# Another order of the attention slot's parts on three engines, and a rearranged prologue

## The chip, the cores and the metric

The kernel runs on one core of a Trainium2 chip. The time is the device time in microseconds of one execution. Five engines run from queues of their own and wait for each other on semaphores: TensorE (PE) does the matmuls into PSUM, VectorE (DVE), ScalarE (ACT) and GpSimd (POOL) work element by element, and SyncE (SP) issues DMAs.

## The reference

It is one transformer-like block on x of shape (2, 1024, 128): attention with 16 heads of 64, a feed-forward layer, a second attention with one head and a distance bias, and the feed-forward layer again. Each has a layer norm ahead and is added to x.

```python
q = einsum('bse,hed->bhsd', x, Wq) + bq      # k, v alike
scores = einsum('bhsd,bhtd->bhst', q, k) / sqrt(64)
scores = where(causal, scores, -inf)
out = einsum('bhst,bhtd->bhsd', softmax(scores), v)
return out.transpose(0, 2, 1, 3).reshape(B, S, H * 64) @ Wo + bo

x = x + attn_a(layernorm(x))
x = x + ffn(layernorm(x))     # relu(x @ w1 + b1) @ w2 + b2
x = x + attn_b(layernorm(x))
x = x + ffn(layernorm(x))
```

## The kernel before

Each engine has its queue written out by hand, and semaphores that only count up tie them together. The order in which the code of an engine stands is the order in which it runs; nothing is reordered.

The change touches the prologue and the first attention. This attention has 32 heads (2 batches x 16), and the kernel goes through one of them in each slot: `pe_slot(u)`, `act_slot(u)` and `dve_slot(u)` say what PE, ACT and DVE do in slot u, for u from 0 to 31; POOL runs `low(u, r)` nine times a slot, and SP moves the pieces. A slot mixes work on several heads:

- scores of head u, `scores(u, r)`: the causal part of the 1024x1024 scores comes in nine units of 512 columns, r = 0 to 8, each in one PSUM bank out of a ring of three. Numbers are split in a high and a low part, so a unit takes two matmuls for each of its parts, and a small one more with the mask where a part lies on the diagonal.
- exponentials of head u, `exponentials(u, r)` on ACT: each unit is read twice, into `p32` in f32 (a ring of four) and into the high part of `p_hl` in f16. POOL subtracts them for the low part (`low`, L1534). `scores` waits for the exponentials three units earlier.
- outputs of head u-1, `products(step)` on PE: nine steps of 12 matmuls, into two groups of four query tiles each; `outputs(0)` and `outputs(1)` on DVE divide the groups by their sums (`outputs_out`). The first group is full after step 2, the second after step 8.
- maxima of head u+1, `maximum(n)`: eight query tiles, the longest (1024 keys) first. PE fills PSUM (`max_tile`, L523) and DVE takes the row maxima (`take_max`, L1126). The five tiles of 512 keys and more come one by one through the same banks, so PE can fill the next only when DVE is done with the one before; the last three alternate between two banks. When all are done, PE turns the maxima (`turn_maxima`, L538) and DVE spreads them into rows of `q_hm` (`max_rows`, L1133), for which the next slot's scores wait.
- a projection for a later pair of heads, `project(half)`: a piece of K or Q, three f32 matmuls of 512 columns into the bank `MISC`; ACT makes the high part (`piece_high`, L911), DVE the low one (`piece_low`, L1109), and SP moves both to their places. Slots 0 to 28 have two pieces each. In slots 1 to 28 a unit of V follows (`value_unit`, `value_high`, `value_low`) in the same bank, behind both pieces.

Of the input's four chunks, two are normalised and turned in the prologue. Chunks 2 and 3, which only heads of the second batch need, are late: `LATE_CHUNKS = (2, 3)`, and `late_chunk(u, step)` gives the chunk whose turn it is in slot u. Their statistics, normalisation (`chunk_norm`, L1094, on DVE), turn on PE (`turn_chunk`, L490) and the split into `xT_hi` (ACT) and `xT_lo` (DVE) stand in the slots. `turn_maxima` also waits for the split of a late chunk, since both use bank 7.

The prologue loads the weights, scales and splits their first quarter, makes pieces 0 to 3 and four units of V, then pieces 4 and 5 (K of the second pair of heads), the maxima of head 0, and, in the middle of them, eight products of a column of bias with Wo (L685). ACT casts and POOL subtracts the other three quarters of the weights; PE waits for that (`rest_lo`) before slot 0. After slot 31 come the output projection, the feed-forward layer, the second attention and the last layer.

## Time and profile before

| | |
|---|---|
| median of 3 runs | 646.46 us |
| lowest, highest | 642.22, 647.32 us |
| the profiled execution | 647.31 us |
| its span in the profile | 645.0 us |
| mean granted clock of PE | 0.957 |
| PE, DVE, ACT, POOL busy | 88%, 75%, 71%, 62% |

The span runs from the first to the last instruction; the execution's own time holds 2.3 us more around it. All rows below are of this one execution, and their times count from the span's start. The busy shares are means over stages of different kinds: prologue to 47.66, slots to about 470, the rest to the end.

### The profile page before, as it was taken

To read this page: it belongs to the slowest core of one execution; us is meant where nothing else is said; L and a number is where in the kernel's file an instruction comes from. 1 tells how busy PE (TensorE), PEld (TensorE's weight loads), DVE (VectorE), ACT (ScalarE), POOL (GpSimd) and SP (SyncE) were. 2 spreads that over 40 slices of the span, in tenths; PEclk is the share of its full clock that TensorE was granted. 3 is DMA by queue.
4 is the path that set the end of the run, shared out by engine and by line. 5 is a ranking of instruction groups with operands and counts; after the bars stand their busy time and mean duration, and the time that the engine had idled before them with its cause. 6 is when DMAs were issued, how large, how long until landed. Compare 5 with 4: busy or idle time off the path is not lost.

```text
span 645.0 us, 16576 instructions
## 1 busy us (share of the span) xinstructions
PE 565.8 (88%) x6230; PEld 414.0 (64%) x6230; DVE 481.3 (75%) x1450; ACT 457.8 (71%) x869; POOL 397.0 (62%) x376
## 2 busy tenths in 40 slices
PE   1668998978999999999999999999799998799697
PEld 1534766645666666766666676666588776577575
DVE  6446878877887787878778887887248799678774
ACT  3447887757878887888888888888745685156375
POOL 3275787856777887788778878888920142045410
PEclk9868999979999999999999999999999999689799
DMA  9422243222322323234233333340754000000001
GB/s 229 98 49 51 51 107 75 66 64 62 96 63 83 91 76 100 58 100 108 51 98 77 90 86 74 85 107 3 246 183 169 0 2 1 0 1 3 1 16 51
DMA packets 35327, 47.88 MB, mean 74 GB/s; under 512 B 10776, under 2 KB 16688, under 8 KB 35248
## 3 DMA queue, kind: packets, MB, share of 16 engines
q1 hardware_dynamic: 33136, 46.29, 26.3%
q8 instruction: 50, 0.82, 0.6%
q10 hardware_dynamic: 2112, 0.54, 0.4%
q14 instruction: 29, 0.24, 0.1%
HBM read 12.21 MB, written 9.44 MB: 34 GB/s over the span
## 4 chain that ended last, share of the span: by engine, by line
PE 35%; ACT 22%; issue 16%; DVE 14%; POOL 10%; DMA 2%; SPq 0%; POOLq 0%; ACTq 0%; DVEq 0%
POOL p_hl L1534 9%; ACT p L975 8%; ACT p_hl L976 7%; PE psum L479 5%; PE psum L481 5%; PE psum L480 4%; PE psum L523 3%; ACT v_all L921 3%; DVE v_all L1116 3%; DVE xn L1094 2%; PE psum L578 2%; PE psum L579 2%; PE psum L558 2%; PE psum L560 2%; PE psum L559 2%
## 5 line engine op out<-in xcount | busy, mean ns | idle before, releaser
L1534 POOL TENSOR_TENSOR p_hl<-p,p_hl 128x512 f16<-128x512 f32 x288 | 326.0, 1161 | 90.5 <-ACT p_hl L976 87.3
L1126 DVE CUSTOM_DVE_ANT_0 max_junk<-psum,mask_s 128x1024 bf16<-128x1024 f32 (+7 forms) x256 | 190.0, 753 | 62.1 <-issue 57.6
L975 ACT ACTIVATE p<-psum 128x512 f32<-128x512 f32 x288 | 179.4, 623 | 16.7 <-PE psum L581 13.4
L976 ACT ACTIVATE p_hl<-psum 128x512 f16<-128x512 f32 x288 | 181.2, 629 | 0.0
L523 PE MATMUL psum<-k_hh,q_hl 128*128 128x512 f16 (+3 forms) x384 | 108.2, 338 | 31.0 <-DVE maxima L1126 30.7
L558 PE MATMUL psum<-v_all,p_hl 128*128 128x65 f16 x1152 | 125.5, 193 | 3.6 <-POOL p_hl L1534 3.6
L559 PE MATMUL psum<-v_all,p_hl 128*128 128x64 f16 x1152 | 125.6, 193 | 0.0
L578 PE MATMUL psum<-q_hl,k_hh 128*128 128x512 f16 (+3 forms) x384 | 125.1, 330 | 0.3 <-DVE q_hm L1133 0.2
L560 PE MATMUL psum<-v_all,p_hl 128*128 128x65 f16 x1152 | 125.1, 195 | 0.0
L579 PE MATMUL psum<-q_hm,k_l 128*128 128x512 f16 (+3 forms) x384 | 123.0, 329 | 0.0
L558 PEld LDWEIGHTS psum<-v_all,p_hl 128*128 128x128 f16 x1152 | 107.9, 99 | 11.9 <-POOL p_hl L1534 4.0
L559 PEld LDWEIGHTS psum<-v_all,p_hl 128*128 128x128 f16 x1152 | 107.1, 98 | 8.0
L560 PEld LDWEIGHTS psum<-v_all,p_hl 128*128 128x128 f16 x1152 | 107.2, 97 | 0.0
L911 ACT ACTIVATE st_hi<-psum,b_kq 128x512 f16<-128x512 f32 x64 | 44.1, 689 | 73.3 <-PE psum L481 63.4
L523 PEld LDWEIGHTS psum<-k_hh,q_hl 128*128 128x128 f16 x384 | 29.1, 98 | 64.5 <-DVE maxima L1126 57.7
L1109 DVE SCALAR_TENSOR_TENSOR st_lo<-psum,b_kq,st_hi 128x512 f16<-128x512 f32 x64 | 47.9, 748 | 26.6 <-ACT st_hi L911 26.6
L578 PEld LDWEIGHTS psum<-q_hl,k_hh 128*128 128x128 f16 x384 | 37.7, 98 | 34.3 <-ACT p_hl L976 15.6
L581 PE MATMUL psum<-mask_t,ident_b 128*128 128x128 bf16 x256 | 53.5, 221 | 0.0
L479 PE MATMUL psum<-xT_hi,w_hi 128*128 128x512 f32 x96 | 46.4, 483 | 5.7 <-DVE w_lo L1247 3.5
L1489 POOL TENSOR_SCALAR var_eps<-mean_var 128x4 f32<-128x4 f32 x16 | 5.4, 340 | 73.3 <-DVE mean_var L1083 73.3
L579 PEld LDWEIGHTS psum<-q_hm,k_l 128*128 128x128 f16 x384 | 37.9, 99 | 8.8 <-issue 0.3
L1575 POOL TENSOR_TENSOR p_hlb<-p32b,p_hlb 128x512 f16<-128x512 f32 x18 | 21.0, 1173 | 35.4 <-ACT p_hlb L1068 35.4
(184 smaller groups left out, 1131.8 us busy)
## 6 DMA issues: line engine op xcount, KB each, us to landing
k_hh<-st_hi SPq DMA_DIRECT2D x64, 128.0 KB, 2.4
o_scratch<-o_sb SPq DMA_DIRECT2D x16, 512.0 KB, 3.1
o_in<-o_scratch SPq DMA_DIRECT2D x4, 2048.0 KB, 7.9
k_l<-st_lo SPq DMA_DIRECT2D x32, 128.0 KB, 2.4
q_hl<-st_hi SPq DMA_DIRECT2D x32, 128.0 KB, 2.3
q_hl<-st_lo SPq DMA_DIRECT2D x32, 128.0 KB, 2.3
q_hm<-st_hi SPq DMA_DIRECT2D x32, 128.0 KB, 2.3
x_sb<-in_L_attn_a_x SPq DMA_DIRECT2D x4, 256.0 KB, 4.1
```

Source lines behind the costliest of these rows:

```text
L479: nc.tensor.matmul(dst, hi, m_hi, start=start, stop=False)
L523: last = nc.tensor.matmul(max_banks(j, c0, c1), q_hl[:, s, P * j:P * (j + 1)], k_hh[:, s, c0:c1], start=True, stop=True)
L558: nc.tensor.matmul(dst, p_hl[:, par, 0, cols], v_hi_one, start=(kt == 0), stop=False)
L559: nc.tensor.matmul(dst[:, 0:DH], p_hl[:, par, 0, cols], v_lo, start=False, stop=False)
L560: last = nc.tensor.matmul(dst, p_hl[:, par, 1, cols], v_hi_one, start=False, stop=(kt == j))
L578: nc.tensor.matmul(dst, k_hh[:, s, keys], q_hl[:, s, q0:q0 + n], start=True, stop=False)
L579: last = nc.tensor.matmul(dst, k_l1[:, s, keys], q_hm[:, s, q0:q0 + n], start=False, stop=not diagonal)
L581: last = nc.tensor.matmul(dst[:, 0:P], ident_b[:, :], mask_t[:, :], start=False, stop=True)
L975: nc.scalar.activation(p32[:, ring_at(u, r), :], src, ACT.Exp, scale=SCALE_A).then_inc(exp_done, 1)
L976: nc.scalar.activation(p_hl[:, u % 2, 0, BANK * r:BANK * (r + 1)], src, ACT.Exp, scale=SCALE_A).then_inc(phi_done, 1)
L1126: nc.vector.tensor_tensor_reduce(out=max_junk[:, n % 2, 0:cols], in0=max_banks(j, 0, cols), in1=mask_s[:, S - cols:S], scale=1.0, scalar=- ...
L1534: nc.gpsimd.tensor_tensor(p_hl[:, u % 2, 1, cols], p32[:, ring_at(u, r), :], p_hl[:, u % 2, 0, cols], ALU.subtract)\
```

## The change

- The order of the parts within `pe_slot`, `act_slot` and `dve_slot` is another. On DVE `max_rows` now stands ahead of `outputs(1)`, and `outputs(0)` ahead of maximum 2.
- The late chunks are normalised on ACT: x times rstd plus a shift of -mean times rstd, which POOL makes (`chunk_shift`). Statistics come in slots 1 and 2, POOL's part in 2 and 3, `late_norm` in 4 and 5, turn and split in 5 and 6 (before: statistics at the starts of slots 4 and 5, normalisation at those of 6 and 7, turn and split in 6 and 7).
- In the prologue, the bias products stand behind the units of V and go to bank 6; pieces 4 and 5 stand between maxima 1, 2 and 3 of head 0; on ACT their high parts come behind the four units of V. SP loads the late chunks of x ahead of the feed-forward weights.

```diff
@@ -356,7 +358,7 @@
 
             return min(u + FIRST_UNITS, VUNITS)
 
-        def late_chunk(u, step=4):
+        def late_chunk(u, step=3):
 
             return u - step if u - step in LATE_CHUNKS else None
 
@@ -400,12 +402,12 @@
             sp.dma_start(w_raw[:, 2, :].rearrange("p (h d) -> p h d", h=H), Wv.rearrange("h e d -> e h d")).then_inc(wv_in, 16)
             sp.dma_start(wo_raw[:, :, :], Wo.rearrange("(k p) e -> p k e", p=P)).then_inc(wo_in, 16)
             sp.dma_start(bo_sb[:, :], bo.unsqueeze(1)).then_inc(bo_in, 16)
+            load_x(2)
+            load_x(3)
             sp.dma_start(w1_raw[:, :], w1).then_inc(ffn_in, 16)
             sp.dma_start(w2_raw[:, :, :], w2.rearrange("(m p) e -> p m e", p=P)).then_inc(ffn_in, 16)
             sp.dma_start(b1_sb[:, :], b1.rearrange("(m p) -> p m", p=P), allow_slow_non_contiguous=True).then_inc(ffn_in, 16)
             sp.dma_start(b2_sb[:, :], b2.unsqueeze(1)).then_inc(ffn_in, 16)
-            load_x(2)
-            load_x(3)
 
             sp.wait_ge(piece_lo, 2)
             move_k(0)
@@ -546,6 +548,7 @@
                         if j == 0:
                             pe.wait_ge(v_lo_done, units_for(w))
                             pe.wait_ge(v_one, 1)
+                            pe.wait_ge(bo_done, 1)
                         if j == 0 or need_units[j] > need_units[j - 1]:
 
                             pe.wait_ge(plo_done, NU * w + need_units[j])
@@ -614,36 +617,36 @@
                         turn_maxima(u + 1)
 
                 products(0)
+                products(1)
                 maximum(0)
-                products(1)
                 project(0)
                 scores(u, 0)
+                scores(u, 1)
                 maximum(1)
-                scores(u, 1)
+                products(2)
                 scores(u, 2)
                 project(1)
                 maximum(2)
-                products(2)
                 products(3)
-                products(4)
-                products(5)
-                maximum(3)
                 scores(u, 3)
                 scores(u, 4)
+                maximum(3)
                 scores(u, 5)
                 value_unit()
                 maximum(4)
-                products(6)
                 maximum(5)
+                products(4)
+                products(5)
                 scores(u, 6)
                 maximum(6)
+                products(6)
                 if late_chunk(u) is not None:
                     pe.wait_ge(v_lo_done, units_after(u))
                     turn_chunk(late_chunk(u))
+                scores(u, 7)
+                maximum(7)
                 products(7)
-                maximum(7)
                 products(8)
-                scores(u, 7)
                 rows()
                 scores(u, 8)
 
@@ -669,22 +672,18 @@
                 if m < 3:
                     pe.wait_ge(piece_lo, m + 2)
                 values(m, V_BANKS[m])
-
-            for n in range(4, 6):
-                pe.wait_ge(piece_lo, n)
-                piece(n, MISC)
+            pe.wait_ge(wo_in, 16)
+            for k in range(OB):
+                last = nc.tensor.matmul(bank(6)[:, 0:1], wo_raw[:, k, :], b_cols[:, 2, k:k + 1], start=(k == 0), stop=(k == OB - 1))
+            last.then_inc(bo_full, 1)
+
             pe.wait_ge(k_moved[0], 48)
             pe.wait_ge(q_moved[0], 48)
             for n in range(QT):
                 max_tile(0, n)
-                if n == 3:
-
-                    pe.wait_ge(wo_in, 16)
-                    pe.wait_ge(piece_lo, 6)
-                    for k in range(OB):
-                        last = nc.tensor.matmul(bank(MISC)[:, 0:1], wo_raw[:, k, :], b_cols[:, 2, k:k + 1], start=(k == 0), stop=(k == OB - 1))
-                    last.then_inc(bo_full, 1)
-            pe.wait_ge(bo_done, 1)
+                if n in (1, 2):
+                    pe.wait_ge(piece_lo, n + 3)
+                    piece(n + 3, MISC)
             turn_maxima(0)
             pe.wait_ge(rows_ready, 1)
             pe.wait_ge(tri_ready, 2)
@@ -899,6 +898,16 @@
                 c = n % CHUNKS
                 nc.scalar.copy(xT_hi[:, BANK * c:BANK * (c + 1)], xt_bank(n)).then_inc(xt_hi_done, 1)
 
+            def late_norm(n):
+
+                act.wait_ge(shift_done, n - LATE_CHUNKS[0] + 1)
+                act.wait_ge(xt_full, n - 1)
+                for j in range(CT):
+                    tile = CT * n + j
+                    last = nc.scalar.activation(xn[:, n % 2, j, :], x_sb[:, tile, :], ACT.Identity, bias=shift[:, tile:tile + 1],
+                                                scale=rstd[:, tile:tile + 1])
+                last.then_inc(xn_ready, 1)
+
             def piece_high(n, src=MISC):
 
                 pair, which, half = n // 4, n % 4 // 2, n % 2
@@ -950,9 +959,8 @@
                 act.wait_ge(v_full, m + 1)
                 nc.scalar.copy(p32[:, m, :], bank(V_BANKS[m])).then_inc(v32_done, 1)
                 value_high(m, V_BANKS[m])
-                if m == 1:
-                    for n in range(4, 6):
-                        piece_high(n)
+            for n in range(4, 6):
+                piece_high(n)
             for which, dst in enumerate((w_hi[:, 0, :], w_hi[:, 1, :], wv_hi[:, :])):
                 act.wait_ge(rest_scaled, which + 1)
                 nc.scalar.copy(dst[:, FIRST:], w_raw[:, which, FIRST:]).then_inc(rest_hi, 1)
@@ -983,9 +991,11 @@
 
                 project(0)
                 exponentials(u, 0)
-                project(1)
                 exponentials(u, 1)
                 exponentials(u, 2)
+                project(1)
+                if late_chunk(u, 2) is not None:
+                    late_norm(late_chunk(u, 2))
                 exponentials(u, 3)
                 exponentials(u, 4)
                 if unit_in(u) is not None:
@@ -1168,27 +1178,25 @@
                         outputs_out(u - 1, g)
 
                 maximum(0)
+                if late_chunk(u, -1) is not None:
+                    first_stats(late_chunk(u, -1))
                 project(0)
                 maximum(1)
+                outputs(0)
                 maximum(2)
                 project(1)
                 maximum(3)
-                outputs(0)
                 maximum(4)
+                maximum(5)
                 if unit_in(u) is not None:
                     value_low(unit_in(u))
-                maximum(5)
+                if late_chunk(u) is not None:
+                    chunk_low(late_chunk(u))
                 maximum(6)
                 maximum(7)
-                if late_chunk(u) is not None:
-                    chunk_low(late_chunk(u))
-                outputs(1)
                 if u + 1 < HEADS:
                     max_rows(u + 1)
-                if late_chunk(u, 1) is not None:
-                    first_stats(late_chunk(u, 1))
-                if late_chunk(u, 3) is not None:
-                    chunk_norm(late_chunk(u, 3))
+                outputs(1)
 
             nc.vector.memset(minus_half[:, :], -0.5).then_inc(half_ready, 1)
             nc.vector.memset(ones[:, :], 1.0).then_inc(ones_ready, 1)
@@ -1265,23 +1273,23 @@
             for n in range(2):
                 piece_low(n, FIRST_BANKS[n])
             norm_v()
-            for n in range(2, 4):
-                piece_low(n, FIRST_BANKS[n])
+            piece_low(2, FIRST_BANKS[2])
             gain_v()
+            piece_low(3, FIRST_BANKS[3])
             dve.wait_ge(inv_done, 2)
             first_low(2)
             for which in range(3):
                 rest_scale(which)
-            for n in range(4, 6):
-                piece_low(n)
             dve.wait_ge(tri_ready, 2)
             for n in range(QT):
                 take_max(0, n)
+                if n in (1, 2):
+                    piece_low(n + 3)
                 if n == 5:
 
                     dve.wait_ge(bo_in, 16)
                     dve.wait_ge(bo_full, 1)
-                    nc.vector.tensor_tensor(bo_all[:, :], bank(MISC)[:, 0:1], bo_sb[:, :], ALU.add).then_inc(bo_done, 1)
+                    nc.vector.tensor_tensor(bo_all[:, :], bank(6)[:, 0:1], bo_sb[:, :], ALU.add).then_inc(bo_done, 1)
             dve.wait_ge(diag_ready, 1)
             dve.wait_ge(qm_zeroed, 1)
             max_rows(0)
@@ -1490,6 +1498,14 @@
                 pool.wait_ge(eps_done, n + 1)
                 nc.gpsimd.tensor_tensor(rstd[:, cols], var_eps[:, cols], minus_half[:, :], ALU.pow).then_inc(rstd_done, 1)
 
+            def chunk_shift(n):
+
+                cols = slice(CT * n, CT * (n + 1))
+                nc.gpsimd.tensor_scalar(shift[:, cols], mean_var[:, cols, 0], -1.0, None, ALU.mult).then_inc(mean_turned, 1)
+                pool.wait_ge(mean_turned, n - LATE_CHUNKS[0] + 1)
+                pool.wait_ge(rstd_done, n + 1)
+                nc.gpsimd.tensor_tensor(shift[:, cols], shift[:, cols], rstd[:, cols], ALU.mult).then_inc(shift_done, 1)
+
             pool.wait_ge(half_ready, 1)
             chunk_rstd(0)
             chunk_rstd(1)
@@ -1537,8 +1553,9 @@
             for u in range(HEADS):
                 for r in range(NU):
                     low(u, r)
-                    if r == 4 and late_chunk(u, 2) is not None:
-                        chunk_rstd(late_chunk(u, 2))
+                    if r == 4 and late_chunk(u, 0) is not None:
+                        chunk_rstd(late_chunk(u, 0))
+                        chunk_shift(late_chunk(u, 0))
 
 
             pool.wait_ge(o_ready, NG * HEADS)
```

Where the order moves is shown at three places of steady slots. The same statements stand 2 to 10 lines further down in the changed kernel. On PE, the rows from the first projection of slot 8 on: `w_hi` and `w_lo` are in the projection, L523 (now L525) is a maximum fill, L578, L579 and L581 (now L581, L582 and L584) are the two matmuls and the mask of scores. Before:

```order
L479 MATMUL psum<-xT_hi,w_hi 128x512
L480 MATMUL psum<-xT_hi,w_lo 128x512
L481 MATMUL psum<-xT_lo,w_hi 128x512
L578 MATMUL psum<-q_hl,k_hh 128x512
L579 MATMUL psum<-q_hm,k_l_81 128x512
L581 MATMUL psum<-mask_t,ident_b 128x128
L523 MATMUL psum<-k_hh,q_hl 128x512
L523 MATMUL psum<-k_hh,q_hl 128x384
L578 MATMUL psum<-q_hl,k_hh 128x384
L579 MATMUL psum<-q_hm,k_l_81 128x384
L581 MATMUL psum<-mask_t,ident_b 128x128
```

And now, from the end of the same projection on:

```order
L483 MATMUL psum<-xT_lo,w_hi 128x512
L581 MATMUL psum<-q_hl,k_hh 128x512
L582 MATMUL psum<-q_hm,k_l_82 128x512
L584 MATMUL psum<-mask_t,ident_b 128x128
L581 MATMUL psum<-q_hl,k_hh 128x384
L582 MATMUL psum<-q_hm,k_l_82 128x384
L584 MATMUL psum<-mask_t,ident_b 128x128
L581 MATMUL psum<-q_hl,k_hh 128x128
L582 MATMUL psum<-q_hm,k_l_82 128x128
L584 MATMUL psum<-mask_t,ident_b 128x128
L525 MATMUL psum<-k_hh,q_hl 128x512
L525 MATMUL psum<-k_hh,q_hl 128x384
```

The fill of maximum 1 (512 and 384 columns) stood behind score unit 0, and now stands behind unit 1.

On PE again, the end of the slot, around the last maximum fill (128 columns) and score unit 7 (512 columns and the mask). Before, from the last output matmul of the slot to the turn of the maxima (L538):

```order
L560 MATMUL psum<-v_all,p_hl 128x65
L578 MATMUL psum<-q_hl,k_hh 128x512
L579 MATMUL psum<-q_hm,k_l_81 128x512
L581 MATMUL psum<-mask_t,ident_b 128x128
L538 MATMUL psum<-ident,maxima 8x128
```

And now, from the same unit of scores to the first of the 24 output matmuls that follow:

```order
L581 MATMUL psum<-q_hl,k_hh 128x512
L582 MATMUL psum<-q_hm,k_l_82 128x512
L584 MATMUL psum<-mask_t,ident_b 128x128
L525 MATMUL psum<-k_hh,q_hl 128x128
L561 MATMUL psum<-v_all,p_hl 128x65
```

Score unit 7 stood between the last output group and the turn of the maxima; now it stands ahead of the last fill, and two groups of 12 output matmuls stand between that fill and the turn.

On DVE, the boundary of two slots, from the last maximum to the first of the next head. Before:

```order
L1126 ISA max_junk,maxima<-psum,mask_s 128x128
L1126 ISA maxima 128x1
L1144 RECIPROCAL o_den<-psum 128x4
L1153 TENSOR_TENSOR o_sb<-psum,o_den 128x4x64
L1133 TENSOR_TENSOR q_hm<-psum,neg_diag 8x1024
L1125 MEMSET gate 128x1
L1126 ISA max_junk,maxima<-psum,mask_s 128x1024
L1126 ISA maxima 128x1
L1109 SCALAR_TENSOR_TENSOR st_lo<-psum,b_kq,st_hi 128x512
```

And now:

```order
L1136 ISA max_junk,maxima<-psum,mask_s 128x128
L1136 ISA maxima 128x1
L1143 TENSOR_TENSOR q_hm<-psum,neg_diag 8x1024
L1154 RECIPROCAL o_den<-psum 128x4
L1163 TENSOR_TENSOR o_sb<-psum,o_den 128x4x64
L1135 MEMSET gate 128x1
L1136 ISA max_junk,maxima<-psum,mask_s 128x1024
L1136 ISA maxima 128x1
L1119 SCALAR_TENSOR_TENSOR st_lo<-psum,b_kq,st_hi 128x512
```

The rows `q_hm` of the next head stood behind the second output group (`o_den`, `o_sb`), and now stand ahead of it.

## Rows read from the trace of the kernel before

**Rows 1.** The page, busy us (share of the span) and instructions of an engine.

```profile
PE 565.8 (88%) x6230; PEld 414.0 (64%) x6230; DVE 481.3 (75%) x1450; ACT 457.8 (71%) x869; POOL 397.0 (62%) x376
```

**Rows 2.** Timeline of DVE, runs of `max_rows`: start, duration, engine, line, output, inputs.

```profile
47.66 1.22 DVE L1133 TENSOR_TENSOR q_hm<-psum,neg_diag 8x1024 f16<-8x1024 f32 x1 [0.61 <-PE psum L538]
60.55 1.22 DVE L1133 TENSOR_TENSOR q_hm<-psum,neg_diag 8x1024 f16<-8x1024 f32 x1 [0.37 <-PE psum L538]
...
126.79 1.22 DVE L1133 TENSOR_TENSOR q_hm<-psum,neg_diag 8x1024 f16<-8x1024 f32 x1
147.32 1.22 DVE L1133 TENSOR_TENSOR q_hm<-psum,neg_diag 8x1024 f16<-8x1024 f32 x1
163.01 1.22 DVE L1133 TENSOR_TENSOR q_hm<-psum,neg_diag 8x1024 f16<-8x1024 f32 x1
175.74 1.22 DVE L1133 TENSOR_TENSOR q_hm<-psum,neg_diag 8x1024 f16<-8x1024 f32 x1
...
431.45 1.22 DVE L1133 TENSOR_TENSOR q_hm<-psum,neg_diag 8x1024 f16<-8x1024 f32 x1
442.08 1.22 DVE L1133 TENSOR_TENSOR q_hm<-psum,neg_diag 8x1024 f16<-8x1024 f32 x1
```

**Rows 3.** Timeline of PE in a steady slot; in brackets idle time and releaser.

```profile
202.74 0.48 PE L479 MATMUL psum<-xT_hi,w_hi 128*128 128x512 f32 x1
...
203.53 0.39 PE L578 MATMUL psum<-q_hl,k_hh 128*128 128x512 f16 x1
...
204.02 0.54 PE L523 MATMUL psum<-k_hh,q_hl 128*128 128x512 f16 x2
...
210.55 0.19 PE L558 MATMUL psum<-v_all,p_hl 128*128 128x65 f16 x1
...
210.92 0.32 PE L523 MATMUL psum<-k_hh,q_hl 128*128 128x384 f16 x1
...
211.63 0.19 PE L558 MATMUL psum<-v_all,p_hl 128*128 128x65 f16 x1
...
212.79 0.23 PE L523 MATMUL psum<-k_hh,q_hl 128*128 128x128 f16 x1 [0.63 <-DVE maxima L1126]
```

**Rows 4.** Timeline of DVE: statistics; fifth maximum of a steady slot.

```profile
100.38 0.87 DVE L1079 BATCH_NORM_STATS2 stats<-x_sb 128x6 f32<-128x128 f32 x4
...
210.76 0.69 DVE L1126 CUSTOM_DVE_ANT_0 max_junk<-psum,mask_s 128x512 bf16<-128x512 f32 x1 [0.77 <-issue]
```

**Rows 5.** Timeline of POOL in the steady slot.

```profile
208.25 1.16 POOL L1534 TENSOR_TENSOR p_hl<-p,p_hl 128x512 f16<-128x512 f32 x1 [1.56 <-ACT p_hl L976]
```

**Rows 6.** Chain of waits (start, us, what): normalisations in prologue and slot 6.

```profile
11.46 1.12 DVE xn L1094 x4
...
128.04 4.40 DVE xn L1094 x4
```

**Rows 7.** One window by engines, in slot 6.

```profile
132.00:138.70 6.70, 5.05 (x22) 3.07 (x23) 3.35 (x8) 0.56 (x1) 0.36 (x1) 0.50 0.00 1
```

**Rows 8.** Timeline of ACT in the prologue, a small copy and two scalings.

```profile
8.79 0.18 ACT L925 COPY b_cols<-psum 128x24 f32<-128x24 f32 x1 [2.76 <-PE psum L652]
...
15.88 0.91 ACT L940 ACTIVATE w_hi<-w_raw,gains 128x256 fp32r<-128x256 f32 x2 [1.52 <-DVE gains L1220]
```

**Rows 9.** Timelines of DVE and POOL in the prologue.

```profile
32.17 0.75 DVE L1109 SCALAR_TENSOR_TENSOR st_lo<-psum,b_kq,st_hi 128x512 f16<-128x512 f32 x1 [4.56 <-ACT st_hi L911]
...
35.37 1.22 DVE L1126 CUSTOM_DVE_ANT_0 max_junk<-psum,mask_s 128x1024 bf16<-128x1024 f32 x1
...
45.18 0.69 DVE L1126 CUSTOM_DVE_ANT_0 max_junk<-psum,mask_s 128x512 bf16<-128x512 f32 x1 [2.93 <-issue]
...
41.47 1.83 POOL L1522 TENSOR_TENSOR wv_lo<-w_raw,wv_hi 128x768 fp32r<-128x768 f32 x1
```

**Rows 10.** The tile `wo_raw`: the bias products.

```profile
L685 PE MATMUL psum<-b_cols,wo_raw x16: 319/352/352, 41.2 to 44.3; 128*128 128x1 f32 x16
```

In rows 7, the window's row has start:end and length, then the busy us (and instructions) of PE, of its weight loads, of DVE, ACT and POOL, the granted clock, the DMA share and GB/s. In rows 10, the row of the tile has count, shortest, median and longest in ns, and the first and last start in us.

More of the change, by code:

```diff
@@ L155, in hybrid_block @@
     minus_half = sb("minus_half", [P, CT], F32)
+    shift = sb("shift", [P, TILES], F32)
     ident = sb("ident", [P, P], F32)
@@ L285, in hybrid_block @@
         bn_done, aggr_done, eps_done, rstd_done = sem("bn_done"), sem("aggr_done"), sem("eps_done"), sem("rstd_done")
+        mean_turned, shift_done = sem("mean_turned"), sem("shift_done")
         xn_ready, xt_full, xt_hi_done, xt_lo_done = sem("xn_ready"), sem("xt_full"), sem("xt_hi_done"), sem("xt_lo_done")
```

## Prediction

> **What bounds the kernel now.** I read the page's busy shares first [rows 1]: TensorE (PE) is busy 88% of the span, VectorE (DVE) 75%; ScalarE (ACT) and GpSimd (POOL) less. So no engine fills the span, and the 32 attention slots, more than 400 us of it, have to be read as a cycle. The marks of that cycle are the runs of `max_rows`, one a slot [rows 2]. From 175.74 (the start of slot 9) they stand 12.785 us apart (20 slots in 255.71 us), and slot 8 takes 12.73; slots 1 to 5 take 66.24 together, slot 6 takes 20.53 and slot 7 15.69; slot 29, which like 30 has no projections, takes 10.63.
>
> Inside one steady slot PE works nearly without a gap, except before the eighth maximum tile: a group of 12 output matmuls starts at 211.63, such a group takes 0.37 (210.55 to 210.92), so PE is free at 212.00 and starts the tile at 212.79, when DVE has done its sixth maximum [rows 3]. That is 0.79 us; the row names 0.63 of it. PE's own work is then 12.785 - 0.79 = 12.0 us a slot. DVE idles in the same slot too, 0.77 before the fifth maximum, until PE has filled it behind the values unit [rows 4]. Both wait for each other in turn: the order in the queues decides, not the work.
>
> **Part 1, the new order in steady slots (8 to 28, 21 of them).** Nothing is added or removed, so PE's 12.0 is the floor. I walked the new order by hand, with issue times from start to start [rows 3]: a group of 12 output matmuls 0.37; two score matmuls of 512 columns with the mask 0.49, without it 0.43; a projection 0.79; a maximum fill 0.43 for 1024 columns, less in proportion below; the values unit 0.71 (what is left of 12.0). DVE: rows 1.25, maxima 1.15, 1.0, 0.88, 0.74, 0.62, 0.48, 0.41, 0.36, a piece's low part 0.73, an output group 0.67, all read from starts in the slot that begins at 201.3; a maximum can start 0.22 after its fill's last issue. ACT: 0.96 for two exponentials, 0.69 for a piece's high part. From PE's turn of the maxima at 0: DVE's rows run 0.32 to 1.54, so PE's projection at 1.80 need not wait; DVE's second output group, now behind the rows, ends at 2.24; maximum 0 (filled at 2.0) runs 2.24 to 3.46; PE asks for it at 3.60. The low part waits for ACT and ends at 4.2, maximum 1 ends at 5.3, PE asks at 5.65. The first output group is done at 6.0, maximum 2 runs 6.2 to 7.1, PE asks at 7.2. The second low part ends at 7.9, when the values unit needs it; maximum 3 ends at 8.7, PE asks at 8.7; maxima 4 and 5 end at 10.4, asked for at 11.2; value_low, 6 and 7 end at 11.9, and the next turn is at 12.04. ACT is at most at exponential r when PE asks for r-3, with over 1 us in hand; POOL needs 9 subtractions of 1.12 from start to start, 10.1 (one is shown, 1.16 long, [rows 5]). So I take 12.02 a slot: 21 x 0.77 = **16.2 us less**. The margins at maxima 1, 2, 3 and 7 are 0.1 to 0.3 us or nothing, so the cost of the order is bounded below by 0 and above by what such misses cost where the trace shows them all (rival 3). `max_rows` ahead of `outputs(1)` is what frees the projection; nothing on PE needs the second group before 3.97, where group 1's bank is started anew.
>
> **Part 2, the late chunks (slots 1 to 7, 102.46 us by the marks).** In the old slot 6, DVE's four normalisations take 4.40 us, 1.10 each, where the same four take 1.12 together in the prologue [rows 6]; POOL is subtracting beside them. PE waits for the maxima behind them, and from 132.0 to 138.7 the granted clock is 0.50, the lower level (1.2 GHz) [rows 7]. The slot pays 7.74 over 12.79, slot 7 pays 2.90. The change takes this off DVE. It adds four ACT activations of 128x128 in slots 4 and 5; none is shown, so the bounds are 0.18 each (the 128x24 copy) and 0.46 (half of the two 128x256 scalings, [rows 8]), and I take 0.3, between them by the size: 1.2 us, on an engine that by the walk has over 1 us in hand: 0.1. Statistics and aggregates (0.87 us and 0.3 more on DVE, [rows 4]) now stand in slots 1 and 2 between maximum 0 and the first low part, where the walk has 0.4 in hand: the third fill comes 0.8 late, 12.84 each. Slots 3 and 4: 12.1. POOL's step, which stood in slots 4 and 5, falls in slots 2 and 3 with two small operations more (`chunk_shift`); with its power of 1.04 it was 1.35 long, the new ones lie between 0.1 and 1.04 each; I take 0.3, by its addition of 0.23. That is the 1.9 us that POOL has spare in a slot: nothing, and at the upper bound a backlog that lasts into the next. Slots 5 and 6 have the turn (0.5 us on PE) and the chain PE turn, ACT high part, DVE low part, maxima 6 and 7, all in a row ahead of the rows: slot 6 13.9, and slot 5, where ACT is 0.9 later still, 14.65. Slot 7 is a steady one, 12.0. Sum 2 x 12.84 + 2 x 12.1 + 14.65 + 13.9 + 12.0 = 90.4: **12.0 us less** (slots 8 to 28 are part 1's).
>
> Here one rule is worth weighing. The Trainium skill (SBUF — State Buffer, "Who interferes with whom") says that a VectorE tensor_scalar in a two-port mode and a GpSimd instruction lock each other out for the whole instruction, while ScalarE waits for nobody. The trace agrees on the first half (1.10 against 0.28 us); no row shows the second. If it failed, and the eight activations took 1.10 each, the sum would be some 4 us worse; if it holds, it stands as above.
>
> **Part 3, the prologue and slot 0.** Pieces 4 and 5 stood ahead of the first maximum; DVE waited 4.56 for the first, and maximum 0 ran at 35.37 [rows 9]. Then the eight bias products (two passes each) took PE from 41.2 to 44.6 at the low clock [rows 10], with DVE idle 2.93. Now the products stand behind the values units, which end at about 30.5 (DVE's 32.17, less 0.7 for ACT's part and 0.95 for the piece); they take half of those 3.4 us at the full clock, and maximum 0 runs at about 32.8. Both pieces go between maxima, 1 us more each (fill, ACT, low part in a row). The rows come at 43.3 to 44.2 instead of 47.66. But the casts of the other weights on ACT move behind piece 5, about 2 us later, and POOL's three subtractions behind them, 1.8 each, end at 45 to 45.7 instead of 43.3 [rows 9], and PE waits for them before slot 0. So PE's slot 0 starts about 2 us earlier. That slot ran at the lower level up to 53.4, and its projection now stands ahead of maximum 1 in both queues, which costs it about 1 us. Bounds for both together 1 and 4 less; I take **2.5 less**. The x loads ahead of the FFN weights on SP's queue move them by 1 us, and they are not cast before 39: nothing. The wait for `bo_done` is long met.
>
> **Part 4, slots 29 to 31.** Without projections PE has 9.7 us of work, and the new order asks for the maxima too early. By the same walk: 0.7 of idleness before maximum 1, 0.45 before 2, 0.67 before 4, so 11.5 against 10.63, twice: 1.8 more. POOL (10.1 a slot) then has less backlog into the last slot, about 1 back. **0.8 us more**. The FFN, the second attention and what else follows 472 us are untouched.
>
> **The sum.** -16.2 - 12.0 - 2.5 + 0.8 = -29.9. The profiled execution took 647.31 (span 645.0): 617.4. The median of the runs shown is 646.46, 0.85 under it: **616.6**.
>
> **Rivals.** (1) DVE's thin margins fail in the steady slots: four places with no more than 0.3 in hand, 0.1 late at each, is 12.4 a slot: 21 x 0.4 = 8.4 worse, 625. For it: maximum 3 is asked for at the very moment it is done. Against: a miss at one place gives the next more room. (2) Slots 5, 6 and 29 to 30 cost less than walked (the turn hidden, POOL the bound at 10.1): 5 better, 611.5. (3) On the other side: PE stands at the head of its queue for most maxima in every slot, as my walk has it for slots 29 and 30, 1.85 us a slot. The slot is then 13.87: 21 x 1.85 = 39 and, in slots 1 to 7, 13 on top of the forecast, 668. It decides above 29.9 / 28 = 1.07 us of waits a slot. For it: the old slot 29, without its fillers, has PE wait 0.48 at maximum 1. Against: the projections and the values unit fill just these places. (4) The order does not do what it says, because the slot's length is set by another loop (the ring of four exponentials on POOL): then only parts 2 to 4 are left, 646.46 - 13.7 = 633. Against: POOL waits for ACT in the steady slot, 1.56 at once [rows 5].
>
> **How the numbers follow.** About 1% (6.5 us) is what a measurement of this kernel can tell from no change; the three runs alone span 5.1. Chances: forecast 0.48 (612 to 621), rival 1 0.26 (621 to 631), rival 2 0.12 (605 to 612), rival 4 0.08 (631 to 642), rival 3 0.06 (from 642 up). The range 606 to 630 leaves out rivals 3 and 4 and the ends of the others. Faster by over 1% holds the forecast, rivals 1 and 2 and most of rival 4: 0.92; within 1% 0.04; slower 0.04.
>
> **What would show it.** Marks of `max_rows` 12.0 apart from slot 8 on and no PE wait for a maximum over 0.2 us in it; slots 5 and 6 near 14 with no half clock after 131; four ACT activations at 0.3 us; the first mark at about 45; slots 29 and 30 longer than 10.63. I am wrong if the steady marks stay near 12.8, or if PE's waits for maxima, once a slot now, come up several times in each.

## The result, and the profile after

The changed kernel takes 613.67 us (median of 4 runs, 611.55 to 614.5) against 644.34 (median of 4, 642.04 to 647.32) on the same chip: a ratio of 0.952, 95% interval 0.946 to 0.957. The forecast was 616.6 against 646.46, the median of three runs before: 29.9 less, where the medians here differ by 30.7. The profiled execution took 611.55, with a span of 609.6.

The page of the changed kernel: busy us and share of the span by engine, then the shares of the chain of work that ended last:

```profile
PE 552.8 (91%) x6230; PEld 407.2 (67%) x6230; DVE 470.3 (77%) x1442; ACT 461.7 (76%) x877; POOL 398.5 (65%) x380
...
PE 65%; DVE 10%; issue 8%; ACT 7%; POOL 1%; DMA 1%; SPq 0%; DVEq 0%; ACTq 0%; POOLq 0%
```

The same line on the chain from the page of the kernel before, and the line of the maximum fills in both pages (busy us and mean ns, then PE's idle time just before them and what ended most of it), before and after:

```profile
PE 35%; ACT 22%; issue 16%; DVE 14%; POOL 10%; DMA 2%; SPq 0%; POOLq 0%; ACTq 0%; DVEq 0%
...
L523 PE MATMUL psum<-k_hh,q_hl 128*128 128x512 f16 (+3 forms) x384 | 108.2, 338 | 31.0 <-DVE maxima L1126 30.7
...
L525 PE MATMUL psum<-k_hh,q_hl 128*128 128x512 f16 (+3 forms) x384 | 101.3, 332 | 9.5 <-DVE maxima L1136 7.5
```

The span is 35 us shorter, and the chain now stays on PE for 65% of it, where it was spread before. PE's idle time before the maximum fills has fallen from 31.0 to 9.5 us. The same answer stands in the marks of the slots, the runs of `max_rows` (now L1143), beside those of [rows 2]:

```profile
44.06 1.22 DVE L1143 TENSOR_TENSOR q_hm<-psum,neg_diag 8x1024 f16<-8x1024 f32 x1 [0.57 <-PE psum L540]
57.31 1.22 DVE L1143 TENSOR_TENSOR q_hm<-psum,neg_diag 8x1024 f16<-8x1024 f32 x1 [0.37 <-PE psum L540]
...
106.56 1.22 DVE L1143 TENSOR_TENSOR q_hm<-psum,neg_diag 8x1024 f16<-8x1024 f32 x1 [0.37 <-PE psum L540]
121.19 1.22 DVE L1143 TENSOR_TENSOR q_hm<-psum,neg_diag 8x1024 f16<-8x1024 f32 x1 [0.37 <-PE psum L540]
134.77 1.22 DVE L1143 TENSOR_TENSOR q_hm<-psum,neg_diag 8x1024 f16<-8x1024 f32 x1 [0.37 <-PE psum L540]
146.73 1.22 DVE L1143 TENSOR_TENSOR q_hm<-psum,neg_diag 8x1024 f16<-8x1024 f32 x1 [0.54 <-PE psum L540]
...
397.73 1.22 DVE L1143 TENSOR_TENSOR q_hm<-psum,neg_diag 8x1024 f16<-8x1024 f32 x1 [0.54 <-PE psum L540]
409.12 1.22 DVE L1143 TENSOR_TENSOR q_hm<-psum,neg_diag 8x1024 f16<-8x1024 f32 x1 [0.54 <-PE psum L540]
420.52 1.22 DVE L1143 TENSOR_TENSOR q_hm<-psum,neg_diag 8x1024 f16<-8x1024 f32 x1 [0.54 <-PE psum L540]
```

Slots 8 to 28 take 251.0 us (146.73 to 397.73), 11.95 each. In brackets the roles have changed: before, PE waited for DVE's maxima, and the steady rows of [rows 2] have no wait at all; now DVE idles 0.54 us before the `max_rows` of every steady slot, because PE's turn of the maxima comes later. At the place of [rows 3] where PE stood idle, its timeline in a steady slot now reads:

```profile
204.88 0.38 PE L581 MATMUL psum<-q_hl,k_hh 128*128 128x512 f16 x1
...
205.31 0.22 PE L584 MATMUL psum<-mask_t,ident_b 128*128 128x128 bf16 x1
205.36 0.22 PE L525 MATMUL psum<-k_hh,q_hl 128*128 128x128 f16 x1
205.42 0.19 PE L561 MATMUL psum<-v_all,p_hl 128*128 128x65 f16 x1
...
206.15 0.27 PE L540 MATMUL psum<-ident,maxima 128*8 128x128 f32 x1
```

The last fill follows the score unit without a gap, and the turn of the maxima follows 24 output matmuls (0.73 us) later. In slots 4 and 5, ACT normalises a late chunk; its timeline in the first of them:

```profile
100.79 1.69 ACT L907 ACTIVATE xn<-x_sb,shift,rstd 128x128 f32<-128x128 f32 x4
```

And windows by engines (start:end and length, busy us of PE, PEld, DVE, ACT, POOL, then the granted clock), one from the middle of slot 0 over all other slots and what follows them up to 510.6, two for the longest stretches at PE's lower level after it:

```profile
50.20:510.60 460.40, 446.07 (x5616) 325.49 (x5613) 371.89 (x1167) 390.83 (x754) 348.16 (x323) 1.00 0.32 88
510.70:517.40 6.70, 6.56 (x23) 5.45 (x23) 5.62 (x12) 1.21 (x3) 0.43 (x1) 0.50 0.01 2
524.40:534.60 10.20, 9.01 (x31) 7.89 (x32) 5.13 (x12) 1.74 (x3) 1.16 (x1) 0.50 0.00 0
```

No half clock is left between 50 and 510 us; before there was one at 132.0 [rows 7], and a short one near 466. The parts, read from the marks (us, before and after in the profiled executions):

| stretch | before | after | difference | forecast |
|---|---|---|---|---|
| up to the first mark | 47.66 | 44.06 | -3.60 | |
| slot 0 | 12.89 | 13.25 | +0.36 | -2.5 with the row above |
| slots 1 to 7 | 102.46 | 89.42 | -13.04 | -12.0 |
| slots 8 to 28 | 268.44 | 251.00 | -17.44 | -16.2 |
| slots 29 and 30 | 21.27 | 22.79 | +1.52 | +1.8 |
| the rest, from slot 31 on | 192.28 | 189.08 | -3.20 | -1.0 |
| span | 645.0 | 609.6 | -35.4 | -29.9 |

### The profile page after: what moved, and what is told of

Its sections match the earlier page's. It is cut to its first block, busy times and chain, and to the rows that moved or that the text cites. A ratio compares the mean times of both kernels' runs of the same rounds, so it can differ in the third digit from the quotient of the medians.

```text
span 609.6 us, 16581 instructions
## 1 busy us (share of the span) xinstructions
PE 552.8 (91%) x6230; PEld 407.2 (67%) x6230; DVE 470.3 (77%) x1442; ACT 461.7 (76%) x877; POOL 398.5 (65%) x380
## 4 chain that ended last, share of the span: by engine, by line
PE 65%; DVE 10%; issue 8%; ACT 7%; POOL 1%; DMA 1%; SPq 0%; DVEq 0%; ACTq 0%; POOLq 0%
PE psum L525 8%; PE psum L581 8%; PE psum L582 8%; PE psum L481 7%; PE psum L483 6%; PE psum L482 6%; PE psum L563 5%; PE psum L561 5%; PE psum L562 5%; PE psum L584 2%; PE psum L720 2%; ACT p L983 2%; PE psum L782 1%; DVE xn L1104 1%; ACT p_hl L984 1%
## 5 line engine op out<-in xcount | busy, mean ns | idle before, releaser
L983 ACT ACTIVATE p<-psum 128x512 f32<-128x512 f32 x288 | 177.2, 615 | 18.2 <-PE psum L584 14.2
L984 ACT ACTIVATE p_hl<-psum 128x512 f16<-128x512 f32 x288 | 178.4, 619 | 0.0
L581 PE MATMUL psum<-q_hl,k_hh 128*128 128x512 f16 (+3 forms) x384 | 125.7, 327 | 0.5 <-ACT p_hl L984 0.4
L582 PE MATMUL psum<-q_hm,k_l 128*128 128x512 f16 (+3 forms) x384 | 122.2, 327 | 0.0
L525 PE MATMUL psum<-k_hh,q_hl 128*128 128x512 f16 (+3 forms) x384 | 101.3, 332 | 9.5 <-DVE maxima L1136 7.5
L920 ACT ACTIVATE st_hi<-psum,b_kq 128x512 f16<-128x512 f32 x64 | 45.5, 711 | 34.2 <-PE psum L483 29.7
L581 PEld LDWEIGHTS psum<-q_hl,k_hh 128*128 128x128 f16 x384 | 37.5, 98 | 26.2 <-issue 9.1
L525 PEld LDWEIGHTS psum<-k_hh,q_hl 128*128 128x128 f16 x384 | 26.3, 98 | 42.9 <-DVE maxima L1136 24.6
L481 PE MATMUL psum<-xT_hi,w_hi 128*128 128x512 f32 x96 | 49.5, 516 | 4.6 <-DVE w_lo L1255 3.5
L584 PE MATMUL psum<-mask_t,ident_b 128*128 128x128 bf16 x256 | 53.0, 220 | 0.0
L1143 DVE TENSOR_TENSOR q_hm<-psum,neg_diag 8x1024 f16<-8x1024 f32 x32 | 38.9, 1216 | 16.5 <-PE psum L540 16.5
```

Of the source, the lines that this page charges most:

```text
L481: nc.tensor.matmul(dst, hi, m_hi, start=start, stop=False)
L525: last = nc.tensor.matmul(max_banks(j, c0, c1), q_hl[:, s, P * j:P * (j + 1)], k_hh[:, s, c0:c1], start=True, stop=True)
L581: nc.tensor.matmul(dst, k_hh[:, s, keys], q_hl[:, s, q0:q0 + n], start=True, stop=False)
L582: last = nc.tensor.matmul(dst, k_l1[:, s, keys], q_hm[:, s, q0:q0 + n], start=False, stop=not diagonal)
L584: last = nc.tensor.matmul(dst[:, 0:P], ident_b[:, :], mask_t[:, :], start=False, stop=True)
L983: nc.scalar.activation(p32[:, ring_at(u, r), :], src, ACT.Exp, scale=SCALE_A).then_inc(exp_done, 1)
```

## The experiments

Each kernel ran beside the kernel before on the same chip. A first set takes the change apart.

**The slot order alone.** The three slot bodies of the changed kernel are put into the kernel before; the late chunks keep their old steps and stay on DVE. The end of `dve_slot`:

```diff
...
                 if u + 1 < HEADS:
                     max_rows(u + 1)
+                outputs(1)
                 if late_chunk(u, 1) is not None:
                     first_stats(late_chunk(u, 1))
                 if late_chunk(u, 3) is not None:
                     chunk_norm(late_chunk(u, 3))
```

> The slot order of the change alone (PE, ACT and DVE), with the late chunks normalised on DVE behind the second output group and the prologue as before. Theory: the order is worth its steady slots, 21 x 0.83 = 17.4 us, and 1.5 us are given back in slots 29 and 30; slots 1 to 5 gain some 0.8 each, slots 6 and 7 keep their DVE normalisations and one of them keeps a stretch at the lower clock. So marks 11.95 apart from slot 8 on, and 18 to 20 us less than before in all. Rival (the order gains only together with the late chunks moved, since a slot that starts late would stay late): marks above 12.3 behind slot 7, and under 12 us less.

Measured: 621.49 us against 643.39, a ratio of 0.966 (0.964 to 0.968), so 22 us less. Slots 8 to 28 take 250.77 us, 11.94 each; the rows below are two of its steady marks (DVE's timeline), and with them the normalisation that still stands in slot 6:

```profile
122.47 1.22 DVE L1133 TENSOR_TENSOR q_hm<-psum,neg_diag 8x1024 f16<-8x1024 f32 x1 [0.54 <-PE psum L538]
124.28 3.64 DVE L1094 TENSOR_SCALAR xn<-x_sb,mean_var,rstd 128x128 f32<-128x128 f32 x4
...
239.94 1.22 DVE L1133 TENSOR_TENSOR q_hm<-psum,neg_diag 8x1024 f16<-8x1024 f32 x1 [0.54 <-PE psum L538]
251.88 1.22 DVE L1133 TENSOR_TENSOR q_hm<-psum,neg_diag 8x1024 f16<-8x1024 f32 x1 [0.54 <-PE psum L538]
```

Slots 6 and 7 still take 18.57 and 15.30. The order does not need the other parts: the rival falls, and the 22 us lie 2 above the theory's 18 to 20.

**The late chunks alone.** ACT's normalisation, POOL's shift and the earlier steps, in the old slot order:

```diff
                 exponentials(u, 2)
+                if late_chunk(u, 2) is not None:
+                    late_norm(late_chunk(u, 2))
                 exponentials(u, 3)
```

> The late chunks of the change alone (statistics in slots 1 and 2, POOL's shift, normalisation on ACT in slots 4 and 5, turn and split in 5 and 6), in the slot order and with the prologue of before. Theory: no DVE normalisation of 4.40 us, no PE wait of 3.98 and no lower clock in slots 4 to 7: slots 1 to 7 take 92 to 95 us instead of 102.46, so 8 to 10 us less in all, and the steady marks stay 12.785 apart. Rival (the stall is only moved, to ACT or to the statistics): under 4 us less.

Measured: 638.48 against 643.39, 0.992 (0.989 to 0.994), 5 us less. Slots 1 to 7 take 95.90 instead of 102.46, slots 4, 5 and 6 14.31, 15.48 and 13.93. It lies between both expectations: the stall and the lower clock are gone, but 6.4 us over seven steady slots remain, more than the theory had, in slots 1 and 2 with the statistics (1.1 together) and in 4, 5 and 6 with ACT's operations, turn and split (5.4 together). How much of that each of these takes was not taken apart.

**The prologue alone.** Pieces 4 and 5, the bias products and the loads of x as in the changed kernel, the slots as before; shown is where the pieces go:

```diff
-            for n in range(4, 6):
-                pe.wait_ge(piece_lo, n)
-                piece(n, MISC)
...
                 max_tile(0, n)
+                if n in (1, 2):
+                    pe.wait_ge(piece_lo, n + 3)
+                    piece(n + 3, MISC)
```

> The prologue of the change alone (bias products behind the units of V, pieces 4 and 5 between the maxima, x loads ahead), with the slots of before. Theory: the first mark at 44.1 instead of 47.66 and slot 0 not shorter, so 3 to 3.6 us less; with the two parts before it adds up to the whole change, 30.7 us. Rival (casts and subtractions of the other weights, which now end later, hold slot 0): the first mark early, but slot 0 longer by 2 to 3 us, so 0 to 1 us less.

Measured: 643.11 (10 runs) against 643.39 (13), 0.9985 (0.996 to 1.001): no difference that the times can show. In its profile the first mark stands at 44.44 and slot 0 takes 13.46, so 2.65 us have been gained by the second mark. That does not come back in the times: their interval reaches only to 2.3 us less, and the theory's 3 to 3.6 lie outside it. The rival has the time right (0 to 1 us less), but not its reason: slot 0 is 0.57 longer and not 2 to 3. The gain up to the second mark is no chance of one profile: with the new prologue alone and in the two profiles of the changed kernel this mark lies between 57.3 and 58.4, and in the five profiles with the old prologue between 60.3 and 61.0. Where the times lose it is open.

The three ratios add up to 4.4% less, where the whole change gave 4.8% (4.3 to 5.4) and, in a second comparison below, 4.9% (4.6 to 5.2). By the last mark the three parts are ahead of the kernel before by 22.8, 5.9 and 3.3 us, 31.9 in sum, and the whole change by 32.2: little or nothing more comes from their being together.

**Why DVE's normalisation was slow.** In the kernel before, the form of the late chunks' instruction is changed, not its place. It is an experiment and no repair, since it computes something else:

```diff
...
+                    if n in LATE_CHUNKS:
+                        last = nc.vector.tensor_scalar(xn[:, n % 2, j, :], x_sb[:, tile, :], mean_var[:, tile, 0:1], rstd[:, tile:tile + 1],
+                                                       ALU.subtract, ALU.mult, accum_out=norm_sums[:, tile:tile + 1])
+                    else:
...
```

> The kernel before, with one thing changed: the four DVE normalisations of each late chunk also write an accumulator to a scratch tile that nothing reads, so that they run in a form without the two-port mode; what the second operation then does to the late chunks' values is left open, so the output is not the reference's. Theory (the 1.10 us each in slot 6 are the two-port form waiting for POOL's subtractions): each takes its own 0.3 to 0.4 us at its place, the four together 1.2 to 1.6 us instead of 4.40, slot 6 shrinks from 20.53 to 15 or 16 and the lower clock at 132 is gone. Rival (they are slow for another reason, such as the operands or the place): still about 1.1 each and slot 6 near 20.5.

Measured in one execution (637.98 us): first the instructions of VectorE that write `xn`, by their tile (count, shortest, median and longest in ns, first and last start), then the window of [rows 7]:

```profile
L1099 DVE TENSOR_SCALAR xn<-x_sb,mean_var,rstd x56: 314/340/1190, 11.2 to 616.3; 128x128 f32<-128x128 f32 x56
L1096 DVE TENSOR_SCALAR_CACHE_REDUCE xn<-x_sb,mean_var,rstd x8: 401/405/407, 128.5 to 144.6; 128x128 f32<-128x128 f32 x8
```

```profile
132.00:138.70 6.70, 6.70 (x94) 4.84 (x91) 4.51 (x15) 5.17 (x11) 4.18 (x5) 1.00 0.27 63
```

The new form takes longer than the plain one does in the median (405 against 340 ns), but none of the eight was stretched: the first four start 0.33 us apart, 1.4 us in all instead of 4.40. Slot 6 shrinks from 20.53 to 15.13, slot 7 from 15.69 to 15.12, and the clock in the window is 1.00. So the form of the instruction made the delay, and not its operands or its place. That it needs POOL's subtractions beside it, the traces show in another place. In the last layer of the changed kernel the plain form takes 2.81 us for four while POOL subtracts beside it, and 1.11 for the next four, when it does not (timelines of DVE and POOL):

```profile
561.34 2.81 DVE L1104 TENSOR_SCALAR xn<-x_sb,mean_var,rstd 128x128 f32<-128x128 f32 x4 [0.97 <-POOL rstd L1499]
570.47 1.11 DVE L1104 TENSOR_SCALAR xn<-x_sb,mean_var,rstd 128x128 f32<-128x128 f32 x4
...
561.28 2.27 POOL L1592 TENSOR_TENSOR p_hlb<-p32b,p_hlb 128x512 f16<-128x512 f32 x2
```

The Trainium skill (SBUF — State Buffer, "Who interferes with whom") states that a tensor_scalar in its two-port form and a GpSimd instruction lock each other out, and leaves out of this the form that writes its accumulator. The trace agrees with both: 1.10 and 0.33 us from one start to the next.

The stall of 3.0 us on DVE made 5.4 of the slot, so nearly half of its price came behind it. The form alone gives 5.9 us in slots 1 to 7, nearly what the move to ACT gives in the same old order (6.6).

A second set asks how the order works. **The changed kernel again**, for comparison with the three below.

> The changed kernel again, unaltered, beside the three that follow. Expected: some 30 us less than before, steady marks 11.95 apart, and what follows the last mark at 189 us, moving by a few us with the stretches at the lower clock.

Measured: 613.43 us (6 runs) against 644.69, 0.951 (0.949 to 0.954). The marks are as far apart as in its first profile, 250.95 us for slots 8 to 28.

**The rows behind the output group again.**

```diff
+                outputs(1)
                 if u + 1 < HEADS:
                     max_rows(u + 1)
-                outputs(1)
```

> The changed kernel with one swap taken back: on DVE the second output group stands ahead of the rows of the maxima again. Theory (by the walk, the projection needs those rows 0.15 us after they come; the output group of 0.67 us ahead of them has to wait for the last output matmuls first): the rows come 0.5 us later, PE waits 0.35 a slot at the projection, steady marks 12.3 apart, 8 to 10 us slower than the changed kernel. Rival (the margin is wider than walked, other work fills it): marks under 12.05, the same time.

Measured: 622.79 us, ratio to the kernel before 0.966 (0.963 to 0.969), 9.4 us slower than the changed kernel, as the theory had it. Steady marks are 12.39 apart. DVE's and PE's timelines in it:

```profile
223.12 0.18 DVE L1154 RECIPROCAL o_den<-psum 128x4 f32<-128x4 f32 x1 [0.43 <-PE psum L563]
223.34 0.42 DVE L1163 TENSOR_TENSOR o_sb<-psum,o_den 128x256 f32<-128x256 f32 x1
223.79 1.22 DVE L1143 TENSOR_TENSOR q_hm<-psum,neg_diag 8x1024 f16<-8x1024 f32 x1
...
225.06 0.51 PE L481 MATMUL psum<-xT_hi,w_hi 128*128 128x512 f32 x1 [0.16 <-DVE q_hm L1143]
```

DVE waits 0.43 for the last output matmuls and then makes PE's projection wait for the rows. One swap of two neighbours on an engine that is busy 77% of the time is worth 0.44 us a slot. In the walk the rows are done at 1.54 and wanted at 1.80, 0.3 in hand, and the output group is done at 2.24 and wanted at 3.97, 1.7 in hand.

**Half of the order.** The kernel before, with PE's order from the fifth group of outputs on, and maximum 5 ahead of the V unit's low part:

```diff
                 products(3)
-                products(4)
-                products(5)
                 maximum(3)
...
-                products(6)
                 maximum(5)
+                products(4)
+                products(5)
                 scores(u, 6)
                 maximum(6)
+                products(6)
...
+                scores(u, 7)
                 maximum(7)
+                products(7)
                 products(8)
-                scores(u, 7)
```

> The kernel before with only the second half of the new order: on PE everything from the fifth group of output matmuls on (maximum 3 comes two groups earlier, and two groups stand between maximum 5 and score unit 6, and two between maximum 7 and the turn), and on DVE maximum 5 ahead of the V unit's low part; late chunks, prologue and the first half of the slot as before. Theory (the waits sit in a ring of PE and DVE, and a wait taken away at one place comes back at others unless the whole order fits): the 0.79 us before maximum 7 is gone, but PE now waits 0.35 for the rows at the projection and 0.4 before maximum 3, steady marks 12.7 to 12.8 apart, no gain. Rival (each removed wait is worth itself): marks at 12.0 to 12.3, 10 to 17 us less.

Measured: 651.78 us, ratio 1.011 (1.009 to 1.014): 7 us slower than before, where the theory had no gain and the rival 10 to 17 us less. Steady marks are 13.01 apart. PE's timeline in one slot:

```profile
221.53 0.45 PE L523 MATMUL psum<-k_hh,q_hl 128*128 128x512 f16 x2 [0.34 <-DVE maxima L1126]
...
222.46 0.38 PE L579 MATMUL psum<-q_hm,k_l 128*128 128x512 f16 x1
222.84 0.39 PE L578 MATMUL psum<-q_hl,k_hh 128*128 128x512 f16 x1
...
229.07 0.20 PE L560 MATMUL psum<-v_all,p_hl 128*128 128x65 f16 x1
229.42 0.50 PE L479 MATMUL psum<-xT_hi,w_hi 128*128 128x512 f32 x1 [0.16 <-DVE q_hm L1133]
```

The 0.79 us before maximum 7 are gone. They came back as 0.49 before maximum 3 (the two groups before it start at 220.30 and take 0.74), 0.32 before the projection (0.35 from the matmul before it, where 0.03 is usual) and 0.16 at score unit 5 (0.38 where 0.22 is usual), which is asked for before ACT has read the bank. That is 0.97, 0.2 more than was walked: the wait on ACT had been left out. With PE's own 12.0 that makes 12.97 of the slot's 13.01.

**A refined version.** Three losses that the profile after shows are taken up; the new order stands in the first branch of `dve_slot` and `pe_slot`, the old one in the second:

```diff
+                if projects(u):
...
+                    maximum(6)
+                    maximum(7)
+                    if late_chunk(u) is not None:
+                        chunk_low(late_chunk(u))
+                    if u + 1 < HEADS:
+                        max_rows(u + 1)
+                    outputs(1)
+                else:
...
+                    outputs(1)
+                    if u + 1 < HEADS:
+                        max_rows(u + 1)
...
             for which in range(3):
                 rest_scale(which)
+            for c in LATE_CHUNKS:
+                first_stats(c)
```

> The changed kernel with three places mended that the profile after shows as losses: slots 29 to 31 keep the order of before on PE and DVE (they have no projections to fill the gaps), DVE takes the low part of a turned chunk behind maximum 7 instead of ahead of maximum 6, and the statistics of both late chunks stand in the prologue, in DVE's idle time behind the scaling of the weights. Theory: slots 29 and 30 back at 10.63 each (1.5 us), slots 1 and 2 at 11.95 (1.2 us), slots 5 and 6 shorter by 0.4 to 0.8 each (1.2 us): 3.5 to 4.5 us less than the changed kernel, some 610. Rival (the gains are taken back, in slot 31 by POOL's backlog and in the prologue by DVE): under 1.5 us less.

Measured: 611.23 us, ratio to the kernel before 0.948 (0.945 to 0.951), against 0.951 (0.949 to 0.954) of the changed kernel beside it: 2.2 us in the medians, with intervals that overlap: less than the 3.5 to 4.5 of the theory, more than the 1.5 of the rival. Two of the three repairs hold: slots 1 and 2 take 11.96 and 11.93 (the statistics run at 27.98 to 30.4, in DVE's idle time), slots 5 and 6 14.16 and 13.23. The third does not. Slots 29 and 30 take 11.17 and 10.63, 1.0 less than in the changed kernel, but slot 31, which also has the old order, gives it back, as the rival said. POOL's last runs of subtractions in the first attention show it (its timelines in the kernel before, the changed kernel and this one):

```profile
451.44 15.65 POOL L1534 TENSOR_TENSOR p_hl<-p,p_hl 128x512 f16<-128x512 f32 x14
...
423.79 10.06 POOL L1550 TENSOR_TENSOR p_hl<-p,p_hl 128x512 f16<-128x512 f32 x9 [0.34 <-ACT p_hl L984]
...
413.94 16.79 POOL L1605 TENSOR_TENSOR p_hl<-p,p_hl 128x512 f16<-128x512 f32 x15 [0.54 <-ACT p_hl L1019]
```

They end 14.4, 13.3 and 14.4 us behind the last mark. From the start of slot 29 to this end it is 35.64, 36.12 and 36.18 us: in the last three slots, behind slots in the new order, the old one is worth nothing. POOL then works without a pause, and PE waits for it at the end. Behind POOL's last subtraction the refined version takes 178.7 us against 176.7 of the changed kernel beside it, though nothing was changed there: this window of it, at the lower clock throughout, is 23.8 us long, where the longest in the changed kernel's two profiles are 10.2 and 17.

```profile
509.50:533.30 23.80, 21.16 (x72) 17.11 (x71) 14.94 (x32) 5.05 (x9) 0.00 (x0) 0.50 0.00 1
```

## Why the prediction was right

**What bounds the kernel** was read rightly: the order, not the work. 12.0 us of PE's own work was the floor that the steady slot reached (11.95). The slot order alone gave 22 us, and the kernel with half of it lost 7.

**Part 1, the walk.** Forecast 12.02 a slot, measured 11.95. In the slot whose turn of the maxima is issued at 194.21, maximum 0 starts at 2.11, 1 at 4.14, 2 at 6.15 and 3 at 7.70 behind it; the walk had 2.24, 4.2, 6.2 and 7.9. All differences are early, and so the margins of nothing at maximum 3 held: between 207 and 219 us PE's timeline names no wait at all. That `max_rows` ahead of `outputs(1)` frees the projection was shown by taking it back (0.44 us a slot; 0.35 walked). That waits come back elsewhere was shown by the half order. The term was 1.2 us too small, by 0.06 a slot.

**Part 2, the late chunks.** Forecast 12.84 for slots 1 and 2, 12.1 for 3 and 4, 14.65, 13.9 and 12.0; measured 12.50, 12.61, 11.95, 12.19, 14.63, 13.58 and 11.96. What each pays for was confirmed where it was tested: statistics out of slots 1 and 2 bring them to 11.95, and the stretched normalisation is the two-port form beside POOL. The term is named after the late chunks, but about half of it is the order: the order alone shortens slots 1 to 7 by 6.8 us, the late chunks alone by 6.6. The size of ACT's operation was off: four take 1.69, 0.42 each, where I took 0.3 (the upper bound, half of 0.91 for two scalings, was 0.46). Each is 0.54 long, no shorter than a scaling of 128x256, so going by the size of the tile was the mistake; why it is so long was not tried. It cost little: slot 4 is 0.24 longer than a steady one. None of the eight was stretched beside POOL's subtractions (0.537 to 0.551 us), so the 4 us of the other case do not arise. POOL's two shift operations take 0.24 and 0.20, by the rows of the tile `shift`, where I took 0.3 each.

**Part 3, the prologue.** Maximum 0 runs at 32.90 (forecast 32.8), the rows come at 44.06 (43.3 to 44.2), POOL's third subtraction ends at 45.51 (45 to 45.7), and the bias products take 1.7 us of PE, from 30.42 to the next fill at 32.12 (half of 3.4). These rows show it, timelines of DVE, POOL and PE in the changed kernel:

```profile
32.90 1.23 DVE L1136 CUSTOM_DVE_ANT_0 max_junk<-psum,mask_s 128x1024 bf16<-128x1024 f32 x1
...
43.72 1.79 POOL L1538 TENSOR_TENSOR wv_lo<-w_raw,wv_hi 128x768 fp32r<-128x768 f32 x1
...
30.42 1.84 PE L677 MATMUL psum<-b_cols,wo_raw 128*128 128x1 f32 x16
32.12 0.59 PE L525 MATMUL psum<-k_hh,q_hl 128*128 128x512 f16 x2
```

PE's slot 0 starts 1.8 us earlier (about 2 forecast), when that subtraction has ended, as the prediction had it. Up to the second mark it is 3.2 us in the profiled executions (2.5 forecast). The 1 us that the new order was to cost slot 0 did not come: with the order alone slot 0 takes 12.88, before 12.89. In the times the part by itself is not seen, so this term rests on profiles alone.

**Part 4, slots 29 to 31.** Forecast 11.5 for slots 29 and 30, measured 11.40, and about 1 us back from POOL's backlog, measured 1.0 (its last subtraction ends 13.3 us behind the last mark, before 14.4). From the start of slot 29 to that end it is 0.5 us more (0.8 forecast).

**Behind the slots.** The rest of the kernel was said to be untouched. Behind POOL's last subtraction it is 2.2 us shorter in these two executions, and this was no step of mine. In the ten profiles of this study that time lies between 174.1 and 178.7 us, and goes with the length of the stretches at the lower clock behind the last mark: 174.1 with 19 us of them (the accumulating form), 175.8 with 21 (the changed kernel), 176.7 with 25 (the same again), 177.9 with 28 (the kernel before), 178.7 with 35 (the refined version). What sets where they fall was not tried. It is part of why the profiled spans differ by 35.4 and the medians by 31: the execution profiled before is the slowest of its four, the one after the fastest of its four.

**The sum.** Up to the last mark the terms were together 3.3 us too small in the profiled executions (32.2 measured, 28.9 forecast). That the medians differ by 30.7, next to the forecast 29.9, is in part luck.

**The rivals.** Rival 1 (thin margins) and rival 4 (another loop) fell with the marks at 11.95. Rival 2 found little: slot 6 costs 0.3 less than walked, slots 29 and 30 0.1 each, slot 5 nothing, 0.5 of its 5 us. Rival 3's mechanism is real: in slot 29 of the changed kernel PE waits 0.39, 0.28 and 0.50 us for maxima, and in the half order 0.34 is named before maximum 3. Slots 29 and 30 differ from the steady ones by having no projections and no V unit.

## What to carry to other kernels

Where several engines hand each other work in a ring, none is full, and the profile names one short wait per round: walk a round with start-to-start times from the trace, all engines beside each other, before moving anything. The named wait is not what is to be won: taken away by half of the new order it came back in three other places and the kernel got slower, while an order that fits reached the floor of the busiest engine. (A smaller edit, such as score unit 7 alone ahead of maximum 7, was not tried.) Look for the instruction with the least time in hand (here the rows that the next projection reads) and put it ahead of neighbours that nobody waits for. And follow a repair to where its stage ends: the old order in the last rounds won 1.0 us in two of them and lost it in the third, where another engine's backlog came due.

## What the runs showed of the hardware that was not expected

- An f32 tensor_scalar of 128x128 on VectorE that also writes an accumulator took 0.40 to 0.41 us beside GpSimd's subtractions, all eight times; the plain one takes 0.34 in the median and up to 1.19 beside them.
- A ScalarE activation of 128x128 from SBUF with bias and scale from tiles takes 0.54 us, 0.39 to the next, also beside GpSimd's subtractions; one of 128x512 from PSUM takes 0.62, 0.48 to the next.
